# Routing of a second mixture of experts inside the steps of the attention layer before it

## What is computed

```python
# third layer, x normalised before it; 8 heads, HD = 16
Wh = (h @ W).reshape(b, n, H, HD).transpose(0, 2, 1, 3)
e = (Wh @ a1)[:, :, :, None] + (Wh @ a2)[:, :, None, :]
e = jnp.where(adj == 0, -jnp.inf, e)
e = jnp.where(e >= 0, e, 0.2 * e)
x = x + softmax(e, -1) @ Wh
# fourth layer, xn = normalised x; 8 experts
probs = softmax(xn @ Wr + br)
top_p, top_idx = top_k(probs, 2)
weights = top_p / top_p.sum(-1, keepdims=True)
h = gelu((layernorm(xn) * ln_g[e] + ln_b[e]) @ W1[e] + b1[e])
x = x + sum_k weights[k] * (h @ W2[e_k] + b2[e_k])
```

## Time and profile before

| | us |
|---|---|
| three executions | 1995.98, 1997.35, 2000.24 |
| median | 1997.35 |
| the profiled execution, its own time | 1992.1 |
| its span from first to last instruction | 1990.4 |
| busy over the span: PE, DVE, ACT, POOL | 1183.0, 1126.9, 999.4, 902.6 |
| second attention, first DMA to last result | 786.5 to 1388.8 |
| routing phase, first DMA to first DMA of the experts | 1389.8 to 1647.8 |

### The profile page before, as it was taken

The page is one execution under the profiler, slowest core; times in us unless marked ns, Lnnn a source line. Parts: engine busy times, 40 slices in busy tenths (PEclk is TensorE's granted clock), DMA queues, the critical chain, the costliest instruction groups (busy, mean ns, idle before and its releaser), DMA issues. The chain is left out here.

```text
span 1990.4 us, 29802 instructions
## 1 busy us (share of the span) xinstructions
PE 1183.0 (59%) x10155; PEld 1014.7 (51%) x10155; DVE 1126.9 (57%) x2519; ACT 999.4 (50%) x1416; POOL 902.6 (45%) x717
## 2 busy tenths in 40 slices
PE   4788776514678750476657657775321207999970
PEld 3777666513556540365445546654321206999860
DVE  4777775632333324599889889998333122333323
ACT  4666665313444420586766766793321205666630
POOL 1005544663556660223523523541566762666650
PEclk8888888756877775688888887888555557999985
DMA  7733331115444416222212212220211125555518
GB/s 237 250 118 128 133 130 46 41 49 168 125 122 145 119 55 192 86 74 83 70 61 81 74 58 83 86 73 15 46 36 36 46 100 167 162 168 165 159 54 253
DMA packets 166116, 213.60 MB, mean 107 GB/s; under 512 B 29812, under 2 KB 121102, under 8 KB 164944
## 3 DMA queue, kind: packets, MB, share of 16 engines
q1 hardware_dynamic: 147792, 175.99, 28.4%
q0 software_dynamic: 18176, 35.72, 5.2%
HBM read 156.71 MB, written 58.56 MB: 108 GB/s over the span
## 5 line engine op out<-in xcount | busy, mean ns | idle before, releaser
L555 POOL DMA_INDIRECT y_dram<-f_ys,f_Xb x312 | 330.4, 1059 | 249.9 <-DVE f_ys L576 166.5
L1485 ACT ACTIVATE g_near<-g_s_row,g_steep 128x1024 fp8e4<-128x1024 f32 x352 | 369.3, 1134 | 2.4 <-issue 2.4
L1460 PE MATMUL g_bp<-g_G,g_near 128*128 128x102 bf16 x4096 | 246.9, 233 | 176.5 <-DVE g_near L1377 176.5
L1460 PEld LDWEIGHTS g_bp<-g_G,g_near 128*128 128x128 fp8e4 x4096 | 239.0, 112 | 204.5 <-issue 203.0
L622 PE MATMUL f_ops<-f_w,f_g 128*128 128x128 f32 x1872 | 276.5, 290 | 64.1 <-issue 35.5
L204 POOL DMA_INDIRECT xs_dram<-r_row,r_pos x256 | 263.9, 1031 | 108.2 <-issue 77.6
L622 PEld LDWEIGHTS f_ops<-f_w,f_g 128*128 128x128 f32 x1872 | 260.0, 204 | 87.1 <-issue 39.1
L658 ACT ACTIVATE f_g<-f_hps,f_ex 128x512 f32<-128x512 f32 x234 | 160.6, 688 | 193.8 <-PE f_hps L614 107.8
L1377 DVE TENSOR_TENSOR g_near<-g_near,g_mask 128x2048 uint32<-128x2048 uint32 x64 | 163.5, 2555 | 50.0 <-ACT g_near L1485 27.5
L1366 DVE TENSOR_SCALAR g_near<-g_s_row,g_nd 128x1024 fp8e4<-128x1024 f32 x160 | 158.3, 1039 | 0.0
L954 PE MATMUL attout<-V,Pt 128*128 128x129 f32 x1024 | 144.4, 300 | 11.7 <-DVE Pt L807 11.6
(11 more groups left out here) (226 smaller groups left out, 2198.7 us busy)
## 6 DMA issues: line engine op xcount, KB each, us to landing
raw<-in_adj SPq DMA_DIRECT2D x64, 512.0 KB, 6.2
g_s_row<-rows_dram SPq DMA_DIRECT2D x64, 512.0 KB, 3.7
f_Xb<-xs_dram SPq DMA_DIRECT2D x78, 288.0 KB
f_w<-in_L_ffn_W SPq DMA_DIRECT2D x78, 256.0 KB
f_yb<-y_dram SPq DMA_DIRECT2D x16, 1024.0 KB, 6.3
f_w<-in_L_ffn_W SPq DMA_DIRECT2D x78, 128.0 KB
mask_dram<-mask SPq DMA_DIRECT2D x16, 512.0 KB, 4.0
g_mask<-mask_dram SPq DMA_DIRECT2D x8, 1024.0 KB
```

The source lines that it names most:

```text
L555: pool.indirect_dma_start(y_d.rearrange("n k d -> (n k) d"), bass.IndirectOffsetOnAxis(ap=Xb[:, i % XB, r, D:D + 1].bitcast(U32), axis=0), ...
L1460: ins = pe.matmul(bp[h % 2][:, t // 4, (t % 4) * 6 * C:(t % 4 + 1) * 6 * C], near[:, h % 4, j, t * P:(t + 1) * P], G[:, s, j, h, :, :], st ...
L1485: ins = act.activation(near[:, h % 4, j, :], s_row[:, h % 4, :], ACT.Relu, scale=STEEP, bias=steep[:, s, j, h:h + 1], saturate=False)
```

## The change

`phase_route` is gone. `phase_gat1` takes the second mixture's routing into its steps, which are now written out with no loop: `route_pipeline` runs steps -1 to 10, and step b also begins the routing of batch r = b-2 and ends that of batch q = b-3. Steps 8 to 10 hold only what is left of the routing. The router's two PSUM tiles are the two halves of the tile for the row products. The partition maximum over a batch is taken from the row products: DVE reduces them along the free axis, scales an 8 x 8 unit matrix by the result, and PE multiplies it by ones, which leaves the 8 maxima in every partition. POOL's split works in place. To make room, near and `s_row` have 3 turns in place of 4, and DVE makes 2 of the 8 blocks in every head (ACT 6). EXPONENTS moves from n = 8 to 9, SCALED from 9 to 10.

```diff
-    BY_DVE = (3, 2) * (NH // 2)
+    BY_DVE = (2, 2) * (NH // 2)
-    near = T("near", [P, 4, NT, N], FP8)
-    s_row = T("s_row", [P, 4, N], FP32)
+    near = T("near", [P, 3, NT, N], FP8)
+    s_row = T("s_row", [P, 3, N], FP32)
-    STATS, NORM, TRANSPOSE, EVAC_XT, PROJECT, EVAC_H, MAXIMUM, EXPONENTS, FACTORS, SCALED, HIGH, MIDDLE = \
-        0, 4, (6, 8), (11, 13), (0, 2, 4), (3, 5, 7), 7, 8, 9, 9, 13, 15
+    STATS, NORM, TRANSPOSE, EVAC_XT, PROJECT, EVAC_H, STEEPNESS, EXPONENTS, FACTORS, SCALED, HIGH, MIDDLE = \
+        0, 4, (6, 8), (11, 13), (0, 2, 4), (3, 5, 7), 7, 9, 9, 10, 13, 15
...
     (SP)
+            R.sp_setup(sp)
...
+                if b == -1:
+                    R.sp_params(sp)
...
-            software_pipeline(sp, step)
+            route_pipeline(step)
+            R.sp_pads(sp)
...
     (POOL)
-            def largest(c):
-                hold(pool, (s_dpm, c + 1))
-                pool.partition_all_reduce(dmax[:, :], dpm[:, :], P, K["rmax"]).then_inc(s_dM, 1)
...
+            def step(b, r, q, done, work, prepare):
+                if b < B - 2:
+                    deviation(b + 2)
+                if b == -1:
+                    R.pool_setup(pool)
+                if 0 <= r < B:
+                    R.pool_roots(pool, r)
+                if q >= 0:
+                    R.pool_gate(pool, q)
                 if done and not ends(b):
                     combine(pool, b - 1, 1 - s)
-                if more(b):
-                    deviation(b + 2)
+                if q >= 0:
+                    R.pool_scatter(pool, q, 0)
                 if done and not ends(b):
                     add(pool, b - 1)
-                if prepare:
-                    largest(b + 1)
+                if q >= 0:
+                    R.pool_scatter(pool, q, 1)
                 if prepare:
                     split(b + 1, 1 - s)
...
     (DVE)
+                if n == LARGEST:
+                    dve.wait_ge(s_e1p, c * 2 + 2)
+                    dve.reduce_max(largest2[:, :], e1_ps[E2, :, :].rearrange("p g n -> p (g n)"), AX.X).then_inc(s_lo, 1)
+                    dve.wait_ge(s_lo, c + 1)
+                    wait(dve, s_mx, c)
+                    dve.tensor_scalar(diag2[:, :], ident[E2, E2], largest2[:, :], None, ALU.mult).then_inc(s_dg, 1)
...
                     if h == 0 and done:
                         sum_parts(b - 1, 1 - s, NH - 1)
+                    if h == 0 and 0 <= r < B:
+                        dve.wait_ge(s_x, r + 1)
+                        R.dve_statistics(dve, r)
                     if h == 1 and ends(b):
                         combine(dve, b - 1, 1 - s)
+                    if h == 1 and 0 <= r < B:
+                        R.dve_shift(dve, r)
+                    if h == 1 and q >= 0:
+                        R.dve_place(dve, q)
...
+                    if h == 6 and 0 <= r < B:
+                        R.dve_choose(dve, r)
...
+            R.dve_table(dve)
...
     (PE)
+                    if h == 3 and prepare:
+                        pe.wait_ge(s_dg, b + 2)
+                        pe.matmul(MX, ones8[:, :], diag2[:, :], start=True, stop=True).then_inc(s_mx, 1)
...
+                    if h == 3 and 0 <= r < B:
+                        pe.wait_ge(s_e1, min(b + 2, B))
+                        pe.wait_ge(s_lo, min(b + 2, B))
+                        R.pe_transpose(pe, r, 0)
+                        R.pe_transpose(pe, r, 1)
+                    if h == 5 and 0 <= r < B:
+                        R.pe_logits(pe, r)
+                    if h == 7 and 0 <= r < B:
+                        R.pe_prefix(pe, r)
...
     (ACT)
                 for h in range(NH):
+                    if h == 0 and q >= 0:
+                        R.act_prefix(act, q)
                     if work:
                         compare(b, s, h)
                     if prepare:
                         prepare_at(b + 1, 1 - s, 2 * h + 1)
                     if more(b):
                         evacuate_at(b + 2, s, 2 * h + 1)
+                    if h == 1 and 0 <= r < B:
+                        R.act_normalise(act, r)
+                    if h == 3 and 0 <= r < B:
+                        R.act_copy(act, r)
+                    if h == 4 and 0 <= r < B:
+                        R.act_evacuate(act, r, 0)
+                        R.act_evacuate(act, r, 1)
+                    if h == 5 and 0 <= r < B:
+                        R.act_logits(act, r)
```

More of the change, by code:

```diff
@@ L27, in hold @@
     eng.nop(nofuse=True)
[L30 to L46, removed]
 RW = 144
@@ L415, in router @@
     R.act_normalise, R.act_copy, R.act_evacuate, R.act_logits, R.act_prefix = act_normalise, act_copy, act_evacuate, act_logits, act_prefix
-    R.s_k, R.s_br, R.s_lgr, R.s_exd = s_k, s_br, s_lgr, s_exd
+    R.s_k, R.s_br, R.s_lgr, R.s_exd, R.s_pf = s_k, s_br, s_lgr, s_exd, s_pf
     return R
[L420 to L479, removed]
 def phase_blocks(nc, sb, pb, sem, K, L, Wr, br, W1, b1, W2, b2, gamma, beta):
@@ L1385, in sum_parts, with step @@
                 dve.wait_ge(s_ap, k + 1)
+                if h == 3 and b < B - 1:
+                    collect_largest(b + 1)
                 dve.reduce_sum(Af[:, s, h, :, :], ap[:, 0:NH * 3 * C].rearrange("p (h s c) -> p h c s", s=3, c=C), AX.X).then_inc(s_Af, 1)
-            def step(b, s, done, work, prepare):
-                if isinstance(b, int) and b == -1:
+            def step(b, r, q, done, work, prepare):
+                s = b % 2
+                if b == -1:
                     normalise_at(0, STATS)
                     normalise_at(0, NORM)
+                if b == 0:
+                    R.dve_setup(dve)
                 for h in range(NH):
@@ L1446, in prepare_at, with step @@
                     ins.then_inc(s_hp, 1)
-            def step(b, s, done, work, prepare):
-                if isinstance(b, int) and b == -1:
+            def step(b, r, q, done, work, prepare):
+                s = b % 2
+                if b == -1:
                     for n in TRANSPOSE:
                         transpose_at(0, n)
+                if b == 0:
+                    R.pe_setup(pe)
                 for h in range(NH):
@@ L1518, in prepare_at, with step @@
                     act.wait_ge(s_rem, c + 1)
-                    act.activation(G[:, f, :, :, 1, :], rem[:, :, :, :], ACT.Copy).then_inc(s_mid, 1)
-            def step(b, s, done, work, prepare):
-                if isinstance(b, int) and b == -1:
+                    act.activation(G[:, f, :, :, 1, :], g32[:, :, :, :], ACT.Copy).then_inc(s_mid, 1)
+            def step(b, r, q, done, work, prepare):
+                s = b % 2
+                if b == -1:
                     for n in EVAC_XT:
                         evacuate_at(0, 0, n)
+                if b == 1:
+                    act.wait_ge(R.s_k, 2)
                 for h in range(NH):
+                    if h == 0 and q >= 0:
+                        R.act_prefix(act, q)
                     if work:
```

137 lines of the change are left out of this document (81 added, 56 removed).

## The result

The changed kernel takes 2013.11 us (median of 6 runs, 2008.64 to 2019.45) where the kernel before took 1995.67 beside it (6 runs): ratio 1.0098, 95% interval 1.0067 to 1.0129. It is slower by 17.4 us. The forecast was 2040, from 1925 to 2090, with slower as the likeliest sign: the sign came, and the change is 0.4 of the 43 us that were forecast over 1997. The profiled execution has a span of 2011.6 us, 21.2 more than before. At the experts' first load 19.5 of them are there (1667.24 against 1647.77).

A forecast was written before the change was run, and what follows sets the result against it. DVE bounds the attention, a POOL chain the routing phase. -176 (tail), -2 (start) and +224 (steps 2 to 7) make +46 on 1992.1: 2038; the median 5 higher, 2043, given as 2040 us, range 1925 to 2090.

The forecast's parts named there:

- Part 1: From step 8's start to the experts' first load: 267.3 us replaced by a routing tail of 91, saving 176.
- Part 2: Start of the second attention: writing out step 1 gains 5, setup and new maximum cost 1 + 2; net -2.
- The loop's term: Step 1 of the attention: written out, it loses ACT's wait for POOL's subtraction and gains 5 us.
- Part 3: Attention steps 2 to 7 with routing: ACT loses its lead at logits and prefix; 635 us against 411.4, +224.
- The placing: DVE's 11 small instructions beside POOL's four combine sums: bounds 0 and 8.8 us held, taken near the upper; ends at 36.3.
- The clock: PE's clock should fall below 0.84, since PE idles ahead of heads 0 and 6.
- the line for head 1: Full step, head 1: DVE's comparisons and masking take turns with POOL's deviation, roots and gate, ending at 25.7 us.
- steps 6 and 7: Last two attention steps: step 6, without moments and normalisation, 106 us; step 7, preparing nothing, 83 us.
- DVE stays the bound: Faster rival, attention steps: handovers cost less, a full step takes 87 us, total 1903; chance 0.30.
- The tail's sets: Rival, routing tail: sets wait for the row buffers, tail up to 20 us longer, total 2060; chance 0.04.
- Starved scatters: Rival, attention steps: each of 16 scatters waits for a whole masking, a set takes 57 us, total 2105; chance 0.04.
- scatters of over 2 us: Sign in POOL's scatters: any lasting over 2 us would prove the prediction wrong.

The follow-up runs named there:

- e5: The kernel before with only the second attention's hardware loop written out: 1970.28 us, ratio 0.9866 to the kernel before.
- e6: The changed kernel with routing taken out of the attention's steps and run as a separate phase again: 1914.19 us, ratio 0.9995 to the kernel before.
- e1: The changed kernel with ACT's copy of the prefix moved behind the blocks of head 0: 1972.45 us, ratio 0.9868 to the kernel before.
- e2: The changed kernel with ACT's logits copy behind head 6 (was 5) and DVE's choosing in head 7 (was 6): 1948.00 us, 0.9743 of the kernel before.
- e3: The changed kernel with prefix copy behind head 0's blocks, logits copy behind head 6 and choosing in head 7: 1911.14 us, 0.9574 of the kernel before.
- e7: The changed kernel with five scratch powers on POOL between first scatters and addition, steps 3 to 6: 1924.50 us, ratio 1.0048 to the kernel before.
- e3b: The changed kernel with prefix and logits copies late and DVE's placing in head 2 instead of 1: 1825.85 us, 0.9531 of the kernel before.

## Where the prediction was right, and the step that failed

- **Part 1 (tail): right.** 91 us forecast, 92.2 measured; saved 175.1 against 176.
- **Part 2 (start): wrong by 3.6 us, hidden by luck.** -2 forecast. From the span's start it looks like -2.2, but 3.8 of that lie in phases that weren't changed; from the attention's first DMA it is +1.6. The loop's term is right by itself: in e5 step 1 gains 5.7 (74.7 to 69.0, masking to masking) and the later steps 6.4. In the changed kernel step 1 gains only 1.1 (73.6), and in e6, without routing, 0.9: the other edits take back nearly 5 in step 1 and 3 in step 0, where I had 3 for setup and maximum.
- **Part 3, mechanism: right.** ACT's lead is lost at the logits and at the prefix. Forecast waits 10 and 14 us, measured 10.7 and 14.0; DVE's ahead of heads 0 and 6 11 and 12, measured 10.8 and 11.3. e1, e2 and e3 removed them, and the time went with them. The placing, taken near its upper bound (36.3 less 25.7 = 10.6), took 9.1 from the gate's end to its own (1088.17 to 1097.26). The clock fell, as said, and the mean masking was 2.35 where I said 2.6.
- **Part 3, size: the step that failed.** +224 forecast, +196.8 measured, 27 us too large; it is why the kernel lost 17.4 us and not 43. Step by step: 110, 112, 112, 112, 106 and 83 against 107.6, 109.1, 109.3, 109.1, 99.6 and 73.4.
- **The term that failed in steps 2 to 5** (11 us together) is the line for head 1 with the placing behind it, "DVE's comparisons, POOL's deviation 1.7 and roots 2.9, masking, gate 1.7 take turns, since each keeps the other out: 25.7". Counted from the end of ACT's copy of the prefix (1064.4), the gate ended at 23.7 and the placing at 32.9, where I had 25.7 and 36.3: 2.0 too much for the turns and 1.4 for the placing. The rest of the step took 76.3 against my 75.7. I had read the power's 3.74 us behind a masking as if the lock held both ways. It holds POOL's power only, as e7 shows.
- **The larger part, 16 us,** is steps 6 and 7 (6.4 and 9.6), which I had given as lumps and not head by head. Some 3 of each are carried over from the line above. I had taken 6 off for step 6; from step 5 to it the trace has 9.5: 4.6 for moments and normalisation, 2.8 in head 1, where the gate no longer stands behind the deviation's power, 1.8 in heads 3 and 4, where the addition holds less, and 0.6 in head 7. Behind the last masking of step 7 no wait for the prefix follows: its sums end 7.5 us after that masking begins, against some 15 us from one masking to the next in the same place before. This is read from the trace; no run tests these two steps.
- **Rivals.** "DVE stays the bound" (87 a step) was false for this kernel and near to what e3 makes of it (88.5, DVE busy for 76.6). The tail's sets did not wait for row buffers. "Starved scatters" did not decide, but I had named scatters of over 2 us as a sign against me, and they came: the mean over the kernel rose from 1031 to 1163 ns, in steps 2 to 7 it is 1.39 us, and 17 of the 80 there took over 2 us (up to 2.74). A scatter that begins inside a masking ends 0.84 to 0.86 us behind it, most of those that follow are back at 0.97; this happens to three of the 16 in each of steps 3 to 7, and POOL's slack of 21.4 us in a full step holds it.

```profile
1108.46 2.29 DVE L1325 TENSOR_TENSOR g_near<-g_near,g_mask 128x2048 uint32<-128x2048 uint32 x1
1108.86 2.73 POOL L185 DMA_INDIRECT xs_dram<-r_row,r_pos  x1 [0.30 <-issue]
...
1111.90 0.97 POOL L185 DMA_INDIRECT xs_dram<-r_row,r_pos  x1 [0.30 <-issue]
```

```profile
L185 POOL DMA_INDIRECT xs_dram<-r_row,r_pos x256 | 297.7, 1163 | 113.8 <-issue 76.1 <-DVE r_pos L294 37.5
```

## What to carry to other kernels

When work moves into the shadow of another stage, price the order of each engine's queue before its load: two copies of 0.22 us, ahead of six blocks of comparisons, cost 20 us a step with no engine busy for more than 72% of it. Put an instruction that waits for the slowest neighbour behind the work that others need next. A held instruction that is cured gives its time back only where nothing else waits in the same heads: e3b cured 8.7 us and gained nothing until two more positions were moved. And unroll before judging: here it gave 1.3% alone, which the change's other edits used up.

## What was not expected of the hardware

- POOL's power of 8 or 16 columns does not keep DVE out, though DVE's wide instructions stretch it (2.9 to between 3.2 and 4.3 us); POOL's sums of 1088 columns do, and DVE's instructions of 8 to 64 columns with them (0.17 to 2.03 us). Reciprocals (0.20) passed beside a sum.
- Chips differ by 4% on this kernel (1998.73 and 1914.43 us for the kernel before), nearly all of it ahead of the second attention: e3 and e3b, on a slow and a fast chip, reach the masking of head 0 of batch 2 at 974.67 and 899.33 us and take 431.0 and 431.6 for the five steps.
